# The attention gather's VectorE order: the next round's multiplications move between the first four additions, the logits between the last four

## The reference, cut to what matters

```python
el = x @ Wl.T
er = x @ Wr.T
e = el[src] + er[dst]
e = jnp.exp(jax.nn.leaky_relu(e, negative_slope=0.2))
rowsum = jax.ops.segment_sum(e, src, num_segments=N)
w = e / jnp.maximum(rowsum, EPS)[src]
heads = [jax.ops.segment_sum(w[:, hd:hd + 1] * x[dst], src, num_segments=N) for hd in range(H)]
```

## Time and profile before

| what | value |
|---|---|
| median of three runs (lowest to highest) | 7106.12 us (7104.03 to 7115.21) |
| the profiled execution's own time | 7045.45 us |
| its span in the profile | 7043.1 us |
| POOL busy, whole span | 3563.8 us (51%) |
| PE busy | 3443.0 us (49%) |
| DVE busy | 2838.6 us (40%) |
| ACT busy | 1926.4 us (27%) |

### The profile page before, as it was taken

The page is one execution under the profiler, slowest core; times in us unless marked ns, Lnnn a source line. Parts: engine busy times, 40 slices in busy tenths (PEclk is TensorE's granted clock), DMA queues, the critical chain, the costliest instruction groups (busy, mean ns, idle before and its releaser), DMA issues. The chain is left out here.

```text
span 7043.1 us, 79417 instructions
## 1 busy us (share of the span) xinstructions
PE 3443.0 (49%) x13479; PEld 2512.4 (36%) x13480; DVE 2838.6 (40%) x7047; ACT 1926.4 (27%) x4744; POOL 3563.8 (51%) x3729
## 2 busy tenths in 40 slices
PE   3445555445355555557423561244555552307990
PEld 0133333334244444446313451133434331204660
DVE  4644444422144444434422254444444446611222
ACT  0232222222233333332101210244444441112331
POOL 0066666666766666665676774455555551050005
PEclk9577777778777777778766786577777776558995
DMA  2232222223133333332101120011111111233113
GB/s 65 68 89 84 84 85 85 85 84 51 36 91 89 90 90 91 90 87 38 21 1 20 28 32 7 16 21 21 21 21 21 20 21 5 111 113 109 55 55 114
DMA packets 280599, 407.39 MB, mean 58 GB/s; under 512 B 93992, under 2 KB 197766, under 8 KB 280263
## 3 DMA queue, kind: packets, MB, share of 16 engines
q0 software_dynamic: 142720, 275.10, 16.6%
q1 hardware_dynamic: 137798, 131.50, 6.0%
HBM read 323.82 MB, written 81.61 MB: 58 GB/s over the span
## 5 line engine op out<-in xcount | busy, mean ns | idle before, releaser
L1070 PE MATMUL conv_ps<-conv_msg,conv_S 128*128 128x256 f32 x3328 | 1233.4, 549 | 1216.9 <-DMA conv_msg<-relu_xn_table,GI 659.2
L1070 PEld LDWEIGHTS conv_ps<-conv_msg,conv_S 128*128 128x128 f32 x3328 | 934.3, 290 | 1543.4 <-issue 1338.7
L1043 DVE TENSOR_TENSOR ACC<-ACC,conv_ps 128x256 f32 x1664 | 700.1, 421 | 1449.0 <-PE conv_ps L1070 1245.2
L994 POOL DMA_INDIRECT conv_msg<-relu_xn_table,GI x832 | 792.5, 953 | 702.7 <-DMA conv_msg<-relu_xn_table,GI 267.0
L1761 POOL DMA_INDIRECT gat_msg<-attn_table,GI x832 | 789.8, 949 | 602.9 <-DVE gat_M L1907 359.5
L994 POOL DMA_INDIRECT conv_msg<-conv_table,GI x832 | 786.8, 946 | 510.4 <-DMA conv_msg<-conv_table,GI 268.6
L1814 PE MATMUL gat_ps<-gat_M,gat_S 128*128 128x260 f32 x1664 | 645.1, 553 | 637.6 <-DVE gat_M L1907 601.6
L1014 ACT ACTIVATE conv_S<-iota_row,LOC 128x128 f32<-128x128 f32 x1664 | 507.9, 388 | 1019.0 <-PE conv_ps L1070 766.9
L1814 PEld LDWEIGHTS gat_ps<-gat_M,gat_S 128*128 128x128 f32 x1664 | 442.6, 281 | 748.6 <-issue 659.9
L1868 DVE TENSOR_TENSOR ACC<-ACC,gat_ps 128x260 f32 x832 | 351.9, 423 | 679.1 <-DMA conv_table<-mlp_a 427.7
L818 POOL DMA_INDIRECT edges_by_src<-mlp_lanes_pay,mlp_lanes_idx x288 | 342.7, 1190 | 109.7 <-issue 76.8
(11 more groups left out here) (388 smaller groups left out, 5171.4 us busy)
## 6 DMA issues: line engine op xcount, KB each, us to landing
expert_in<-router_zrow SPq DMA_DIRECT2D x53, 256.0 KB
experts_xe<-expert_in SPq DMA_DIRECT2D x106, 128.0 KB
expert_out<-experts_y SPq DMA_DIRECT2D x106, 128.0 KB
conv_msg<-relu_xn_table,GI POOLq DMA_INDIRECT x832
conv_msg<-conv_table,GI POOLq DMA_INDIRECT x832
gat_msg<-attn_table,GI POOLq DMA_INDIRECT x832
relu_xn_table<-norm_rx SPq DMA_DIRECT2D x49, 128.0 KB
xnT<-norm_xt SPq DMA_DIRECT2D x49, 128.0 KB
```

The source lines that it names most:

```text
L994: pool.indirect_dma_start(msg[:, h * RING + k, :], None, table, bass.IndirectOffsetOnAxis(ap=m.GI[:, t:t + 1], axis=0)).then_inc(got[h], 16)
L1043: nc.vector.tensor_tensor(acc, acc, ps[k % NB][:, 0:D], ALU.add).then_inc(added, 1)
L1070: nc.tensor.matmul(ps[k % NB][:, 0:D], S[:, h % 2, k, :], msg[:, h * RING + k, :], start=True, stop=True).then_inc(summed, 1)
```

## The change

VectorE's step gets another order. The four multiplications of round r+1 come first, each followed by one of the additions 0 to 3; then L1881, addition 4, L1888, addition 5, L1895, additions 6 and 7. No instruction is added or removed, and every wait stays beside its instruction.

```diff
             def step(r, h):
                 if there(r):
                     starts = [v.snap(b * AW) for b in bins_of_round(nc, m, DVE, r)]
-                if there(r + 2):
-                    ... (L1881, the reduction of the logits of round r+2, with its waits)
-                if there(r):
-                    add(r, h, 0, starts[0])
-                if there(r + 2):
-                    ... (L1888)
-                if there(r):
-                    add(r, h, 1, starts[1])
-                if there(r + 2):
-                    ... (L1895, lk_made)
-                if there(r):
-                    add(r, h, 2, starts[2])
-                    add(r, h, 3, starts[3])
                 if there(r + 1):
                     g1 = ahead(h, 1)
                     v.wait_ge(e_made, r + 2)
                     held(v, tv)
                     Mg = M[:, g1 * RING:(g1 + 1) * RING, :]
                 for q in range(4):
                     if there(r + 1):
                         last = nc.vector.tensor_tensor(Mg[:, :, 64 * q:64 * q + 64], ...)
                         if q == 3:
                             last.then_inc(m_made, 1)
                     if there(r):
-                        add(r, h, 4 + q, starts[4 + q])
+                        add(r, h, q, starts[q])
+                if there(r + 2):
+                    ... (L1881, with its waits)
+                if there(r):
+                    add(r, h, 4, starts[4])
+                if there(r + 2):
+                    ... (L1888)
+                if there(r):
+                    add(r, h, 5, starts[5])
+                if there(r + 2):
+                    ... (L1895, lk_made)
+                if there(r):
+                    add(r, h, 6, starts[6])
+                    add(r, h, 7, starts[7])
```

More of the change, by code:

```diff
@@ L1872, in step @@
                     starts = [v.snap(b * AW) for b in bins_of_round(nc, m, DVE, r)]
-                if there(r + 2):
[L1874 to L1882, removed]
-                if there(r):
-                    add(r, h, 0, starts[0])
-                if there(r + 2):
-                    v.wait_ge(z_made, r * 2 + 5)
-                    held(v, tv)
-                    nc.vector.tensor_tensor(z, z, msg[:, g * RING:(g + 1) * RING, 64:GW], ALU.add).then_inc(z_made, 1)
-                if there(r):
-                    add(r, h, 1, starts[1])
-                if there(r + 2):
[L1892 to L1896, removed]
-                if there(r):
-                    add(r, h, 2, starts[2])
-                    add(r, h, 3, starts[3])
                 if there(r + 1):
@@ L1911, in step @@
                     if there(r):
-                        add(r, h, 4 + q, starts[4 + q])
+                        add(r, h, q, starts[q])
+                if there(r + 2):
+                    g, half = ahead(h, 2), h % 2
+                    z = zz[:, half, :, :]
+                    v.wait_ge(el_made, r + 3)
+                    v.wait_ge(got[g], landed(r + 2, g))
+                    if later(r + 2, 2):
+                        v.wait_ge(e_made, r + 1)
+                    held(v, tv)
+                    nc.vector.tensor_reduce(z, pel[half][:, 0:12 * RING].rearrange("p (k c q) -> p k q c", c=3, q=4),
+                                            X_AXIS, ALU.add).then_inc(z_made, 1)
+                if there(r):
+                    add(r, h, 4, starts[4])
+                if there(r + 2):
+                    v.wait_ge(z_made, r * 2 + 5)
+                    held(v, tv)
+                    nc.vector.tensor_tensor(z, z, msg[:, g * RING:(g + 1) * RING, 64:GW], ALU.add).then_inc(z_made, 1)
+                if there(r):
+                    add(r, h, 5, starts[5])
+                if there(r + 2):
+                    v.wait_ge(z_made, r * 2 + 6)
+                    held(v, tv)
+                    nc.vector.scalar_tensor_tensor(out=lk[:, half, :, :], in0=z, scalar=0.2, in1=z,
+                                                   op0=ALU.mult, op1=ALU.max).then_inc(lk_made, 1)
+                if there(r):
+                    add(r, h, 6, starts[6])
+                    add(r, h, 7, starts[7])
             staggered(v, step)
```

## The result

The changed kernel takes 7192.32 us (median of three runs, 7183.16 to 7210.01) against 7106.12 us: 1.0122 times the time before, with a 95% interval of 1.0088 to 1.0156. It is slower by 86 us; 84 us less were forecast.

What follows compares the result with a forecast made beforehand. Waits bound the kernel, with PE's late results released only after gather batches. Rounds of 12.4 instead of 13.28 us over 96 rounds take 84 us from 7106, giving 7022 us; range 6830 to 7190 us.

Steps and rivals of the forecast that it cites:

- PE's idling for the multiplications goes: PE's first sum of a round: its 578.4 us wait for DVE's last multiplication should be nearly gone, whatever the time does.
- Batches in pairs: POOL's gathers: two batches follow each other without a pause, a pair of rounds taking 24.8 us.
- the likeliest case: Rounds 4 to 100: joined batches give 12.4 us a round instead of 13.28, 84 us less; chance 0.48.
- The batches' own length: POOL's two joined batches: 9.98 us plus 8.73 us to the start of the second batch's last gather.
- the release comes 2.89 us after the last gather: End of a pair: held PE results come free 2.89 us after the last gather's start, 21.6 us into the pair.
- the batch starts at F + 3.2: DVE's tail: after F, the release of held results, additions 0 to 2 and multiplications take 3.2 us before POOL's next batch.
- The time from the last gather before a pause to ACT's copy should stay 2.9 us: ACT's copy of the transposes: still 2.9 us after the last gather before a pause, as in the profile before.
- `lk_made` later costs nothing: DVE's later signal to ACT's exponential: covered by ACT's one-hots; 0.3 us might show, nothing was taken.
- The base: Rounds 4 to 100: 13.28 us each, from an execution of 7045.45 us; 60.7 us to the median carried over.
- Multiplications beside gathers cost nothing: DVE's multiplications at the start of a batch: 0.684 us with gathers, 0.681 without, so no cost.
- The tail grows on each round: Slower rival: sums held in every batch, `m_made` only after release, 14.8 us a round, 148 us more; slower overall 0.27.
- POOL becomes the bound: Faster rival: lateness goes, gathers set the round at about 10.2 us, 296 us less, 6810 us; chance 0.15.

Runs made afterwards that it cites:

- third chip: Holding chip, kernel before 7047.45 us: changed kernel 1.0144, early multiplications alone 1.0116, late logits alone 0.9971, changed with POOL released by the last addition 1.0035.
- second chip: Both recorded kernels rerun unaltered where results are held: kernel before 7102.86 us, changed kernel 7188.72 us, ratio 1.0109.
- the fourth: Chip that holds nothing: kernel before 6725.77 us, unaltered changed kernel 6730.23 us, ratio 1.0006; one gather a round 6380 us.
- fifth chip: Holding chip, kernel before 7112.73 us: changed kernel with POOL waiting for the previous batch's landing 6977.21 us, ratio 0.981; with one gather a round 6432.12 us.
- before_paced: Kernel before, with POOL also waiting until the whole previous batch of gathers has landed: 6920.14 us, ratio 1.0298, on a chip that holds nothing.
- before_split: Kernel before, with POOL waiting in each batch after four gathers for the fourth's landing: 6830.46 us, ratio 1.0169, on a chip that holds nothing.

## Why the prediction was wrong, point by point

- *PE's idling for the multiplications goes*: right, 578.4 us to nothing that the waits view lists.
- *Batches in pairs*: right, 48 waits of POOL in 96 rounds. In the likeliest case that was the mechanism, and its price is where the forecast failed.
- *The batches' own length*, 9.98 + 8.73 = 18.71 us: 18.91 us.
- *"the release comes 2.89 us after the last gather"*: 4.01 us, 1.1 us more a pair.
- *"the batch starts at F + 3.2"*: this step failed; it was 7.08 us, 3.9 us more a pair. Its ground was "At F PE has been let run ahead, so sums 0 to 3 of the next round r are among them". In the trace additions 2, 3 and 4 of the running round came out one at a time, at 4933.47, 4938.42 and 4948.39, 5 and 10 us apart, so F met addition 4 of that same round. Nor could PE run ahead, since each sum needs the bank that the addition four tiles earlier frees: the next matmuls after additions 2 and 3 start at 4934.05 and 4938.99. Additions 4 to 7 with the logits between them stand first, 3.30 us from 4948.39 to the first multiplication; then three pairs of multiplication and addition and the last multiplication, 3.78 us to the batch. I had counted the second part alone. Together with the release this makes 24.8 us into 29.8 us; 30.0 us were measured.
- *"The time from the last gather before a pause to ACT's copy should stay 2.9 us"*: it didn't. In the changed kernel the copy is queued behind the exponential and starts at 4950.28, 5.90 us after the last gather.
- *`lk_made` later costs nothing*: wrong within pairs. The exponential waited 799.3 us in all, up to 16.3 us, and it stands in the tail in front of the multiplications. The third chip prices the late logits beside early multiplications at 26 us, while alone they gave 21 us.
- *The base.* I took 13.28 us a round from an execution of 7045 us and carried 60.7 us over to the median. On the second chip, at 7103 to 7111 us, a round was 13.88 us: those 60 us lie in this stage too (1332.59 against 1274.50 us). The change made of it 14.80 us.
- *Multiplications beside gathers cost nothing*: right. The group view has this, in minimum, median and maximum:

```profile
L1880 DVE TENSOR_TENSOR gat_M<-gat_msg,gat_M x392: 682/685/730, 4601.2 to 6028.3; 128x512 f32<-128x512 f32 x196
```

- *The rival "The tail grows on each round"* named the sign and even the round, 14.8 us. Its mechanism, each batch alone with its own release, is not what happened: the agreement of 14.8 with 14.81 us is luck. *"POOL becomes the bound"* is what the changed kernel does on a chip that holds nothing, at 10.49 us a round, and there the kernel before takes the same total (its trace on such a chip wasn't taken).

That the early multiplications cause the loss is shown (third chip), that the loss is absent where nothing is held is shown on one such chip (the fourth), and that the changed kernel with a pause after each batch is faster than the kernel before, without pairs, is shown where results are held (fifth chip). Not shown: whether the kernel before would gain as much from the pause on a chip that holds, since before_paced never met one; what holds the results, and whether the recording has a part in it; and what lets them out, since before_split met a chip that holds nothing. Before and after, the release comes 2.9 and 4.0 us after the start of the last gather, and paced POOL sees the landing 3.25 us after it (4912.83 to 4916.08); that is nearness in time and no more. The last packets of a batch end 2.1 us after the start of its last gather both before and after the change (medians), so the release doesn't follow them at a fixed distance either: 0.8 and some 2 us.

The rule that the prediction set against the row, in the Trainium skill's page "TensorE: Matmul & The Clock Gate", section "The cost: per-tile semaphore tail" (some 26 ns for an increment on a matmul), fits the fourth chip, where POOL is the bound at 10.49 us a round, and doesn't fit the recorded one, where an addition waits up to 12.3 us.

No version was seen to win on both kinds of chip. The paced changed kernel is 1.9% faster than the kernel before where results are held and 3.1% slower where they aren't; late logits alone give 0.3% where they are held and were not timed where they aren't.

## What to carry to other kernels

When a semaphore is moved forward, look at each listener by itself: one that was kept in step by the old, late signal (here POOL's batches) may run on and lengthen a stall that hangs on its pauses. Price the tail behind a stall from what will be due at its end, which depends on how much came out during the stall, and not from what is due in the old order. And when the trace shows a wait whose named releaser is long done, have the kernel before timed on several chips before costing a change on it.

## What the runs showed of the hardware

- The same program takes 6717 to 6726 us on three chips and 7047 to 7113 us on three others. Most of the gap lies in this stage: for the changed kernel 415 of 483 us (1422.20 against 1006.96 us, spans of 7207.8 against 6724.6 us). Some of the rest is in other stages: the paced and the one-gather kernels, whose rounds are alike on both kinds, still differ by 44 to 60 us in the total (6977 against 6931 to 6934, 6432 against 6372 to 6380).
- On the slower chips an addition waits up to 12.3 us for a result of PE while gathers run, and PE's semaphore events themselves come late; with one gather a round this isn't so. PE's speed doesn't explain it: in the rounds of the changed kernel the granted clock is 0.67 where results are held and 0.80 where they aren't, but PE is busy for 685.23 us and 696.27 us.
- Every trace from the slower chips lacks about half of the semaphore events (46,518 in the recorded trace of the kernel before, 90,408 in the fourth chip's), and no trace from the faster ones does.
- What in a chip makes the difference was not found.
